# A first phase in which another engine normalises the rows, and in another order

## The reference, cut to what matters

```python
x = x + attn(_layernorm(x))        # then cross attention, then the experts

def _layernorm(x, axis=-1, eps=1e-05):
    m = jnp.mean(x, axis=axis, keepdims=True)
    v = jnp.var(x, axis=axis, keepdims=True)
    return (x - m) / jnp.sqrt(v + eps)

# in attn, hs the normalised rows:
q = silu(dwconv(hs @ q_proj_w.T, q_conv_w))      # causal depthwise convolution, 4 taps
k = silu(dwconv(hs @ k_proj_w.T, k_conv_w))
v = silu(dwconv(hs @ v_proj_w.T, v_conv_w))
beta = sigmoid(hs @ b_proj_w.T)
long_ = dwconv(v, fir_long_w)                    # 31 taps; needs the taps in reversed order
```

## Time and profile before

| | us |
|---|---|
| median of three runs | 1255.64 (1254.59 to 1255.67) |
| the profiled execution, its time | 1256.81 |
| its span in the trace | 1254.50 |
| first convolution of group 0 starts on VectorE | 20.08 |
| last convolution of group 7 ends on VectorE | 181.7 |
| TensorE busy over the span | 1079.8 (86%) |
| VectorE busy | 869.7 (69%) |
| GpSimd busy | 561.4 (45%) |
| ScalarE busy | 529.5 (42%) |

### The profile page before, as it was taken

How to read it: one execution, slowest core, us unless ns; L and a number is a source line. 1 busy time by engine, 2 the same in 40 slices (tenths; PEclk the granted TensorE clock), 3 DMA queues, 4 the chain that set the end, 5 groups by cost and what they waited for, 6 DMA issues and landing times.

```text
span 1254.5 us, 24154 instructions
## 1 busy us (share of the span) xinstructions
PE 1079.8 (86%) x8466; PEld 828.0 (66%) x8466; DVE 869.7 (69%) x2268; ACT 529.5 (42%) x968; POOL 561.4 (45%) x998
## 2 busy tenths in 40 slices
PE   4979879698799899899999999899989788877792
PEld 2646558676677677676686687686677666756682
DVE  4898986854676776876766777777778365645477
ACT  4767663405124513522532522432541245734561
POOL 4233435256137636535735824843750233343452
PEclk9999998888899999999999999999999789998996
DMA  6544441441101511320250250130110442323488
GB/s 168 176 132 143 128 146 68 160 119 30 56 1 44 166 52 43 112 100 27 70 164 1 72 182 2 60 124 1 60 68 6 148 174 85 93 89 102 128 267 304
DMA packets 86789, 127.56 MB, mean 102 GB/s; under 512 B 28304, under 2 KB 62608, under 8 KB 84496
## 3 DMA queue, kind: packets, MB, share of 16 engines
q1 hardware_dynamic: 79472, 106.30, 27.2%
q0 software_dynamic: 7200, 19.74, 4.3%
HBM read 66.47 MB, written 59.55 MB: 100 GB/s over the span
## 4 chain that ended last, share of the span: by engine, by line
PE 46%; DVE 17%; POOL 17%; issue 8%; ACT 6%; another core or an unknown queue 3%; DMA 2%; SPq 0%; ACTq 0%; DVEq 0%; POOLq 0%
PE bank L696 7%; POOL arena L1451 6%; POOL arena L1453 6%; DVE arena L1581 5%; PE bank L508 3%; PE bank L762 2%; PE bank L666 2%; PE bank L548 2%; PE bank L752 2%; PE bank L914 2%; POOL orn L1468 2%; PE bank L562 2%; PE bank L675 2%; ACT arena L1083 2%
## 5 line engine op out<-in xcount | busy, mean ns | idle before, releaser
L988 ACT ACTIVATE arena<-bank 128x512 f32<-128x512 f32 (+2 forms) x358 | 187.1, 540 | 453.2 <-PE bank L574 123.8
L1515 POOL DMA_INDIRECT results<-arena x78 | 76.5, 980 | 104.8 <-DVE arena L2138 78.6
L1581 DVE SCALAR_TENSOR_TENSOR arena<-arena,param 128x512 f32<-128x512 f32 x144 | 106.0, 751 | 23.1 <-ACT arena L1011 19.7
L1451 POOL TENSOR_TENSOR arena<-arena 128x126 f32<-128x126 f32 (+22 forms) x217 | 91.3, 421 | 37.7 <-DVE arena L1681 22.2
L696 PEld LDWEIGHTS bank<-arena 128*128 128x128 f32 x768 | 92.9, 199 | 5.3 <-issue 4.3
L1453 POOL TENSOR_TENSOR arena<-arena 128x126 f32<-128x126 f32 (+22 forms) x217 | 87.0, 401 | 17.0
L1435 POOL COPY arena<-arena 32x128 f32<-32x128 f32 x128 | 51.7, 404 | 95.1 <-DVE arena L1671 89.2
L696 PE MATMUL bank<-arena 128*128 128x128 f32 x768 | 93.8, 283 | 0.0
L914 PE MATMUL bank<-arena 128*128 128x128 f32 x624 | 88.4, 288 | 0.2 <-ACT arena L1260 0.2
L410 PE MATMUL bank<-const,arena 128*128 128x128 f32 x256 | 41.8, 316 | 53.4 <-DVE arena L1555 41.2
L1387 POOL DMA_INDIRECT slots_x<-arena x64 | 63.0, 984 | 49.2 <-DVE arena L1877 31.9
(11 more groups left out here) (273 smaller groups left out, 2688.7 us busy)
## 6 DMA issues: line engine op xcount, KB each, us to landing
arena<-slots_x SPq DMA_DIRECT2D x78, 129.0 KB
slots_x<-rows_of_no_token SPq DMA_DIRECT2D x8, 1161.0 KB
xt<-x_in SPq DMA_DIRECT2D x16, 512.0 KB, 5.0
kq_T<-kq SPq DMA_DIRECT2D x8, 1024.0 KB, 3.8
kq<-kq_T SPq DMA_DIRECT2D x8, 1024.0 KB
arena<-results SPq DMA_DIRECT2D x32, 256.0 KB
arena<-ffn_in SPq DMA_DIRECT2D x7, 768.0 KB, 4.2
vT<-v_T SPq DMA_DIRECT2D x8, 514.0 KB
```

The costliest lines, as they stand in the source:

```text
L988: free(act.activation(out_, in_, func, **kw), name)
L1451: own.link(pool.tensor_tensor(tmp, rows32[:, m0:, k].unsqueeze(2).broadcast_to([P, nm, k]), units[:, 0:k, k].unsqueeze(1).broadcast_to([P, ...
L1515: pool.indirect_dma_start(results[:, :], bass.IndirectOffsetOnAxis(ap=dest[:, n % YS:n % YS + 1], axis=0), ys[:, n % YS, :], None).then_in ...
L1581: ins = V.scalar_tensor_tensor(cv[:, k % 4, :], pre[:, j, d:d + GT], param[:, at + d:at + d + 1], cv[:, k % 4, :], ALU.mult, ALU.add)
```

## The change

Four things are done.

1. The rows are normalised on GpSimd, by four instructions of the same form (`tensor_scalar`, subtract and multiply). Each counts up `hs_rows_ready`, so that TensorE and SyncE wait for 4 per group. GpSimd makes groups 0 and 1 ahead of the reversal of the taps, and group i + 1 in its step i from i = 1 on.
2. VectorE makes the statistics of group i + 1 at the head of group i, before convolution 0, also for i = 0. Since `mv[0]` is one buffer, it waits there until GpSimd has made the rows of group i.
3. VectorE no longer makes rows. Convolutions 1 to 5 follow each other.
4. On SyncE, a group's eight tap loads now come after the store of its transposed rows and the load of the rows two groups on. The wait for the reversed taps, their store and the wait for its landing move from ahead of group 0 into group 0, behind these two.

```diff
-    "hs_stats_ready": 1, "hs_rstd_ready": 1, "hs_rows_ready": 1, "hs_stored": 16, "halo_ready": 1,
+    "hs_stats_ready": 1, "hs_rows_ready": T, "hs_stored": 16, "halo_ready": 1,
...
             def hidden_rows(i):
-                pe.wait_ge(sem("hs_rows_ready"), i + 1)
+                pe.wait_ge(sem("hs_rows_ready"), T * (i + 1))
...
-            norm_scale(0, "hs", 1)
+            def hidden_rows(i):
+                pool.wait_ge(sem("hs_stats_ready"), i + 1)
+                own.link(pool.tensor_tensor(rstd[0][:, :], mv[0][:, :, 1], eps[:, 0, 0:T], ALU.add))
+                own.link(pool.tensor_tensor(rstd[0][:, :], rstd[0][:, :], minus_half[:, 0:T], ALU.pow))
+                if i:
+                    drained(pool, f"hsT0.{i - 1}")
+                    drained(pool, f"hsT1.{i - 1}")
+                for t in range(T):
+                    done(pool.tensor_scalar(xn_hs[:, t, :], xt[:, i % G, t, :], mv[0][:, t, 0:1], rstd[0][:, t:t + 1],
+                                            ALU.subtract, ALU.mult), "hs_rows_ready")
+
+            hidden_rows(0)
+            hidden_rows(1)
             reverse = prm("fir_l").rearrange("p (c j) -> p c j", c=CK)
...
             for i in range(NG):
-                if i + 1 < NG:
-                    norm_scale(0, "hs", i + 2)
+                if 0 < i < NG - 1:
+                    hidden_rows(i + 1)
                 if i:
                     rnorm(i - 1)
...
             def hidden_stats(i):
                 dve.wait_ge(sem(f"x{i % G}_loaded"), 16 * (i // G + 1))
+                if i:
+                    dve.wait_ge(sem("hs_rows_ready"), T * i)
                 norm_stats(0, xt[:, i % G, :, :], "hs")
...
             hidden_stats(0)
             halo(0)
-            hidden_rows(0)
...
             for i in range(NG):
+                if i + 1 < NG:
+                    hidden_stats(i + 1)
                 conv(i, 0)
...
-                if i + 1 < NG:
-                    hidden_stats(i + 1)
-                conv(i, 1)
-                if i + 1 < NG:
-                    hidden_rows(i + 1)
-                for j in range(2, 6):
+                for j in range(1, 6):
                     conv(i, j)
...
-            sp.wait_ge(sem("taps_reversed"), 2 * FL - 1)
-            sp.dma_start(taps_d.rearrange("c p w e -> p c w e"), ext).then_inc(sem("taps_stored"), 16)
-            sp.wait_ge(sem("taps_stored"), 16)
...
             for i in range(NG):
                 b, g = divmod(i, G)
-                for q in range(4 * i, 4 * i + 4):
-                    load_taps(q)
                 for c in range(CK):
                     drained(sp, f"hsT{c}.{i}")
                 done(sp.dma_start(hs_d[i, :, :, :], hsT_b[i % 2][:, :, :]), "hs_stored", 16)
-                sp.wait_ge(sem("hs_rows_ready"), i + 1)
+                sp.wait_ge(sem("hs_rows_ready"), T * (i + 1))
                 if i + G < NG:
                     load_rows(i + G)
+                if i == 0:
+                    sp.wait_ge(sem("taps_reversed"), 2 * FL - 1)
+                    sp.dma_start(taps_d.rearrange("c p w e -> p c w e"), ext).then_inc(sem("taps_stored"), 16)
+                    sp.wait_ge(sem("taps_stored"), 16)
+                for q in range(4 * i, 4 * i + 4):
+                    load_taps(q)
```

More of the change, by code:

```diff
@@ L1561, in hidden_stats @@
                 dve.wait_ge(sem(f"x{i % G}_loaded"), 16 * (i // G + 1))
+                if i:
+                    dve.wait_ge(sem("hs_rows_ready"), T * i)
                 norm_stats(0, xt[:, i % G, :, :], "hs")
-            def hidden_rows(i):
-                if i:
-                    drained(dve, f"hsT0.{i - 1}")
-                    drained(dve, f"hsT1.{i - 1}")
-                norm_rows(0, xn_hs, xt[:, i % G, :, :], "hs", i + 1)
             def halo(i):
```

## The result

The changed kernel takes 1238.86 us (median of four runs, 1235.70 to 1244.66) against 1255.37 for the kernel before beside it: ratio 0.9883, 95% interval 0.9857 to 0.9909, 16.5 us less. The profiled execution took 1235.70 us, its span is 1233.6.

A forecast was written before the change was run, and what follows sets the result against it. VectorE was taken to bound the kernel. Gains and costs of 12.3 + 10.6 - 0.4 - 1.0 - 0.5 - 4.5 = 16.5 us took 1256.8 to 1240.3, as a median 1239.1 us, range 1233 to 1249.

The forecast's parts named there:

- Statistics, 7 x 1.76: At group borders on VectorE: statistics of 1.76 us fit into the 1.90 round trip, saving 12.3 us over seven sets.
- Rows off VectorE, 7 x 1.51: In seven groups VectorE loses the rows' 1.30 us and the 0.21 wait for rstd, saving 10.6 us.
- The row operation's price, 0.40: One row operation on GpSimd takes 0.40 us, kept between 0.36 and 1.0.
- Startup, 0.4: Four GpSimd row operations ahead of the first transposes replace 1.38 on VectorE, costing 0.4 us (0.1 to 2.8).
- if the first transposes start after 14: Sign at the kernel's start: first transposes later than 14 us would show the prediction wrong.
- Interference, 0.15 per group: GpSimd's row operations hold up VectorE's steps by 0.15 us a group, 1.0 in all (0 to 16).
- Reversal, 18 us long from 20 to 38: GpSimd's 61 tap copies slip between VectorE's steps, two per step, and end at about 38 us (28 to 42).
- Stall at the border of groups 1 and 2, 4.5: VectorE waits 4.5 us (3.7 to 5.1) for group 3's rows, loaded behind the late taps in SyncE's queue.
- Behind the phase nothing changes: After the first phase all stays as before, so the whole gain of 16.5 us was expected to last to the end.
- Rival 3: Slower than before if GpSimd's operation holds VectorE 0.95 us or more; about 1265 us at 1.3. Chance 0.06.
- Rival 4: TensorE takes over: half-clock stretches in each group raise its 16.76 us to 18.4, costing 6.6, time 1245.7. Chance 0.06.
- The rule weighed in the prediction: Each GpSimd row operation costs VectorE its full length; in the rival with this or dearer operations, 1247 to 1255, chance 0.12.

The follow-up runs named there:

- all_rows_dve: The changed kernel with all rows made on VectorE again, behind convolution 1; 1206.66 us against 1222.61 for the kernel before, ratio 0.9879.
- rows_plus_one: The changed kernel with tile 0's row operation made twice on GpSimd in groups 2 to 7; 1217.15 us against 1222.05 for the kernel before.
- stats_late: The changed kernel with the statistics of groups 2 to 7 back behind the transposes of v; 1261.14 us against 1222.61 for the kernel before.
- first_rows_dve: The changed kernel with group 0's rows made on VectorE again; 1245.84 us against 1256.29 for the kernel before, ratio 0.9921.
- first_rows_late: first_rows_dve with TensorE's transposes of the rows and ScalarE's copies of them one projection later; 1222.00 us against 1222.05 for the kernel before.
- reversal_first: first_rows_dve with the reversal of the taps ahead of group 1's rows on GpSimd; 1239.68 us against 1256.29 for the kernel before, ratio 0.9857.
- sync_order_alone: The kernel before with SyncE's new order alone, rows and statistics unmoved; 1256.25 us against 1256.29 for the kernel before, ratio 1.0002.

## Why the prediction came out right, point by point

The total is 0.2 us from the forecast (1238.86 against 1239.1), and that closeness is luck twice over. At the phase's end 14.2 us were gained where the steps had 16.5, and the median made up the rest from a part that the change doesn't touch; on the other chip the gain was 11.3. And within the phase errors cancelled: 3.5 lost at the start and 2.2 in the rows against 3.0 won back at the stall and 0.5 in the copies, 16.5 - 5.7 + 3.5 = 14.3. What is right by its mechanism is the statistics' term. Interval by interval, before less after: start -3.85, groups 0 to 6 +2.87, +0.65, +2.99, +2.85, +3.18, +2.52, +2.96, group 7 0.0.

- **Statistics, 7 x 1.76.** Right. They fit into the round trip; all_rows_dve, which has this and keeps the rows on VectorE, has groups of 18.6 where the earlier trace rows has 20.7, 2.0 less (the wait of 0.21 for rstd goes too).
- **Rows off VectorE, 7 x 1.51.** They are off it, but less came of it. The 0.21 for rstd goes with the early statistics already; of the other 1.30 the interference leaves 0.85 per group, where the prediction's own terms leave 1.15.
- **The row operation's price, 0.40.** The step that failed. The prediction took it from the copy, as the nearest in form. It is 1.21 alone and up to 1.75 beside VectorE, outside the bounds of 0.36 to 1.0. I took the prices of a copy with as many elements and of a two-input operation as its bounds, and both were right for what they are (0.39 and 0.61). Neither says anything of the form with scalars (0.91 to 1.22). The power, named there as a hint that forms differ, was the better hint.
- **Startup, 0.4.** 3.85, of which 4.85 - 1.38 = 3.47 is the price again. (By the prediction's own price it should have been 4 x 0.40 - 1.38 = 0.2.) It calls itself wrong "if the first transposes start after 14": they started at 16.03, so this sign of being wrong came true and did name the failing step.
- **Interference, 0.15 per group.** 0.42 to 0.46: 15 steps take 11.63 to 11.67 in groups with rows, 11.21 without (11.44 of the last row above, with its block of 0.23). In most groups just three steps carry it, 0.85, 0.93 and 0.86 us where the others take 0.75. Three times as much as predicted, but for operations three times as long: per microsecond of GpSimd's work it is 0.07 us, less than the 0.38 (0.23 of 0.60) of the earlier trace rows. The step of 0.93 in each group touches a second of the prediction's signs of being wrong (steps of 0.9 and more in every group), though only one step in 18 shows it.
- **Reversal, 18 us long from 20 to 38.** 18.1 long, from 24.14 to 42.20: the length was right, the start late by the rows. Two copies pass per step, as the last section shows. Their own cost to VectorE, 0.5 in the prediction, is nothing: each of the 15 steps beside them took 0.75. For an end at 42 the prediction priced the stall at 8.5.
- **Stall at the border of groups 1 and 2, 4.5.** 1.5. The taps landed 1.8 us after their store was issued, not 7.1. From there the load of group 3's rows was issued at 53.1 and landed after 7.4 us, not 5.2, at 60.5. VectorE, delayed by the start, wanted the rows only at 59.1, not at 54.4. So two errors, the store's and the start's, made up for the late reversal. The 7.1 of before was no price of this store: it stood right behind four small stores of zeros, which landed at 21.8, 25.1, 26.6 and 28.3, and landed itself at 28.8.
- **Behind the phase nothing changes.** Right for the 819 us of the middle. The experts' part differs from run to run by more than the phase's errors, which is enough for 14.2 in the phase to be 16.5 in the medians on one chip and 11.3 on another.
- **Rival 3, slower by a dear operation.** Its price held (1.2 to 1.75 is beyond its 0.95) and its result didn't. The result rested on exclusion, that VectorE loses (p - 0.17) for each operation met, and VectorE lost some 0.4 for 5.80 us of them. The path that does limit it is one I had seen but priced with the wrong numbers ("ready at 4 to 5 us", "rows by 7.8 hold nobody up"): the rows are ready at 8.3, TensorE waits, and with 1.45 more (rows_plus_one) VectorE waits too. The change stands just short of it.
- **Rival 4, TensorE's clock.** The argument against it holds for the change, where the clock is 1.00 from 55 us on. In stats_late, first_rows_dve, first_rows_late and rows_plus_one the clock was a large part of what decided.

The rule weighed in the prediction, an exclusive lock for the whole instruction (the Trainium skill, page "SBUF — State Buffer", section on the two separate sides), would have cost VectorE some 3.6 us per group, by an estimate from three of the four operations meeting steps at 1.21 each. The trace doesn't agree, with 0.4. It is mostly GpSimd that waits: its row operations grow from 1.23 to 1.64 and 1.75 beside steps. Which part of an instruction excludes the other engine, as the prediction says of reading, no run separates.

## What to carry to other kernels

A price taken from another form of instruction is a price of that form: an operation with scalars on GpSimd cost three copies. Filling a round trip at a group's border with work that was elsewhere on the same engine was the whole gain here, and moving work to a free engine only paid when it didn't stand at the start in front of everything, nor behind other work (the taps' reversal) there. Look for the engine that is next: TensorE has 16.76 us of work in a period of 17.73. Once its wait for an input passed that difference of 1 us, the rest of the wait, and each fall of its clock, went into the phase's time. And a landing time read from a trace belongs to what stood before it in its queue.

## What the runs showed of the hardware

GpSimd's small copies pass two to a VectorE step. Windows of the changed kernel, the first with small VectorE work, the second with 15 convolution steps; columns as above, GpSimd's count is the last one in brackets:

```profile
26.20:28.60 2.40, 2.40 (x7) 1.00 (x6) 2.19 (x8) 1.99 (x4) 2.40 (x13) 1.00 0.94 69
28.70:39.90 11.20, 10.27 (x46) 5.99 (x45) 10.49 (x15) 10.84 (x18) 11.20 (x31) 1.00 0.14 41
```

13 copies in 2.4 us, but 31 in 11.2 us beside 15 steps, about one of each pair lasting as long as the step (the longest is 0.73, the shortest 0.18 us). VectorE's steps don't get longer for it: the longest of these 15 took 0.754 us, as alone. A row operation of 1.23 us grows to 1.75 beside steps that follow transposes, and to 2.27, three steps long, beside steps alone (first_rows_dve). It costs VectorE little: some 0.4 us per 5.80.

A DMA's landing time depends on what stands before it in its queue. The same store of the taps landed after 1.8 us at 42 us in this kernel, and after 7.1 at 22 us in the kernel before, 0.4 behind the last of the four stores of zeros, although the DMA engines moved almost nothing from 24 us on. In reversal_first and sync_order_alone, behind the zeros, the transposed rows and a load of rows, it landed after 8.9 and 9.1 us, again 0.4 behind the load before it.
